# A two-layer block of attention, FP4 feed-forward, Mamba and LoRA: the products of the scan moved from VectorE to TensorE and GpSimd

## The reference

```
A_disc = exp(delta[..., None] * A)
B_x = delta[..., None] * Bm[:, :, None, :] * x1[..., None]
hc = a * hc + b          # a scan over t, for each (d, n)
y = einsum('tbdn,btn->btd', hs, Cm)
```

## Time and profile before

| | |
|---|---|
| median of the three runs | 1017.21 us |
| the profiled execution's own time | 1005.87 us |
| its span | 1003.6 us |
| VectorE busy | 724.7 us, 72% of the span |
| TensorE busy | 692.3 us, 69% |
| ScalarE busy | 461.2 us, 46% |
| GpSimd busy | 153.4 us, 15% |
| chain that ended last | TensorE 37%, VectorE 33%, DMA 11%, ScalarE 8% |

### The profile page before, as it was taken

How to read it: one execution, slowest core, us unless ns; L and a number is a source line. 1 busy time by engine, 2 the same in 40 slices (tenths; PEclk the granted TensorE clock), 3 DMA queues, 4 the chain that set the end, 5 groups by cost and what they waited for, 6 DMA issues and landing times.

```text
span 1003.6 us, 12436 instructions
## 1 busy us (share of the span) xinstructions
PE 692.3 (69%) x4131; PEld 407.2 (41%) x4131; DVE 724.7 (72%) x1295; ACT 461.2 (46%) x931; POOL 153.4 (15%) x265
## 2 busy tenths in 40 slices
PE   3247665786679776877778667956795777855555
PEld 1124344344544444434533454434543453433122
DVE  2716156986789687968897788868896779863951
ACT  2213432662566246634556356625662256436312
POOL 5512013013110412002300230022100000000000
PEclk9997867797889889889979897989898798976775
DMA  4421501361035303350136103520353013002300
GB/s 120 78 54 40 100 1 38 108 139 24 11 99 138 68 0 107 103 103 0 43 120 126 24 11 118 136 48 10 97 133 67 1 47 115 22 0 70 104 0 5
DMA packets 41151, 65.93 MB, mean 66 GB/s; under 512 B 8113, under 2 KB 30338, under 8 KB 38786
## 3 DMA queue, kind: packets, MB, share of 16 engines
q1 hardware_dynamic: 38946, 64.51, 26.0%
q10 hardware_dynamic: 2176, 1.05, 0.6%
HBM read 57.68 MB, written 7.86 MB: 65 GB/s over the span
## 4 chain that ended last, share of the span: by engine, by line
PE 37%; DVE 33%; DMA 11%; ACT 8%; issue 8%; SPq 1%; POOL 0%; DVEq 0%; ACTq 0%
PE ps_s L1052 9%; PE ps_f L1052 8%; DVE shared L1006 6%; PE ps_n L1052 6%; DMA bcrow<-bc_dram 6%; PE ps_y L1052 6%; PE ps_v L1052 6%; DMA x_tm<-in_L_attn_x_dram 5%; DVE mx L893 4%; DVE shared L1000 4%; DVE shared L1011 2%; ACT lmem L757 1%; DVE bn L814 1%; ACT L760 1%; ACT adisc L731 1%
## 5 line engine op out<-in xcount | busy, mean ns | idle before, releaser
L1052 PE MATMUL ps_y<-shared,ident 128*128 128x512 f32 x256 | 146.7, 702 | 52.3 <-DVE shared L1011 52.1
L1052 PE MATMUL ps_s<-stack_mem 72*128 72x128 bf16 (+2 forms) x1280 | 162.9, 248 | 4.8 <-DVE mx L893 4.4
L893 DVE TENSOR_REDUCE mx<-ps_s 128x4 f32<-128x512 f32 x192 | 126.6, 685 | 52.5 <-PE ps_s L1052 49.3
L1006 DVE TENSOR_TENSOR_SCAN shared<-adisc,shared 128x1024 f32<-128x1024 f32 x64 | 146.7, 2292 | 2.2
L1052 PEld LDWEIGHTS ps_s<-stack_mem 72*128 72x128 bf16 (+1 forms) x1280 | 111.1, 106 | 75.6 <-issue 32.0
L649 ACT ACTIVATE probs<-ps_s 128x512 f32<-128x512 f32 x192 | 105.5, 598 | 66.2 <-PE ps_s L1052 64.2
L731 ACT ACTIVATE adisc<-delta,amat 128x255 f32<-128x255 f32 x256 | 108.1, 504 | 39.0 <-DVE shared L1006 28.8
L1052 PE MATMUL ps_s<-causalT,ident_bf 128*128 128x512 bf16 x192 | 83.1, 433 | 23.1 <-DVE mparts L902 14.1
L1000 DVE TENSOR_TENSOR shared<-u,bcrow 128x1024 f32<-128x1024 f32 x64 | 78.0, 1218 | 28.0 <-DMA bcrow<-bc_dram 27.8
L1052 PEld LDWEIGHTS ps_y<-shared,ident 128*128 128x128 f32 x256 | 50.2, 218 | 107.6 <-DVE shared L1011 64.8
L1052 PE MATMUL ps_s<-causal,ident_bf 128*128 128x512 bf16 x128 | 55.3, 432 | 46.7 <-DVE mx L893 36.8
(11 more groups left out here) (213 smaller groups left out, 1114.2 us busy)
## 6 DMA issues: line engine op xcount, KB each, us to landing
bcrow<-bc_dram SPq DMA_DIRECT2D x64, 512.0 KB, 4.2
stack_mem<-stack_dram SPq DMA_DIRECT2D x48, 192.0 KB
stack_mem<-stack_dram SPq DMA_DIRECT2D x144, 64.0 KB
stack_dram<-parts SPq DMA_DIRECT2D x24, 256.0 KB, 2.3
x_tm<-in_L_attn_x_dram ACTq DMA_DIRECT2D x8, 128.0 KB, 11.4
xb<-in_L_attn_x_dram SPq DMA_DIRECT2D x8, 128.0 KB, 2.8
out_dram<-y_out SPq DMA_DIRECT2D x8, 128.0 KB, 2.5
fmem<-in_L_attn_conv_w_dram SPq DMA_DIRECT2D x1, 512.0 KB
```

The lines of the kernel that those rows point to most:

```text
L893: V.tensor_reduce(mx[:, a, i, hd], ps_s[:, n % 2].rearrange("p (h n) -> p h n", n=P), AX.X, ALU.max).then_inc(s_max, 1)
L1006: V.tensor_tensor_scan(hs[:, j % HB].rearrange("p n c t -> p (n c t)"), adisc[:, j % 2].rearrange("p n c t -> p (n c t)"), bx[:, j % 2].re ...
L1052: return nc.tensor.matmul(o, lhsT, rhs, start=start, stop=stop, **kw)
```

## The change

- **u times B.** `mamba` now computes B transposed (tokens on partitions) with six small matmuls, and transposes u by four into `uT`. ScalarE makes, for each state and half of the tokens, a diagonal matrix of B (`diag`, four 128-column activations a step). TensorE multiplies `uT` by the diagonals: 32 fp32 matmuls of 256 columns a turn into `ps_f`, one bank for each half c of the channels (new stream `products`). VectorE scans from PSUM, one instruction of 512 elements for each c, 16 a turn. The product for (j+1, c) waits for the scan of (j, c), as they share the bank.
- **Times C.** One GpSimd product of 1024 elements a step, in place (new stream `scan` on GpSimd). Only C is sent to the partitions, in four DMAs of 512 KB a turn, all issued once the projection is there.
- **Stack.** The 12 loads of the stack's parts per pass become four, each read three times by a broadcast.
- **Maxima and masks.** The first pass takes the second token half against all 256 keys, so that a maximum needs no second operation; the causal matmuls cover only the blocks that need a mask.
- **LoRA.** The 16 token rows go by one DMA to one partition; each correction is four matmuls of one row by one row. GELU reads PSUM with the bias.
- **Smaller ones.** The sum of the two attention outputs is made by TensorE in the transposes; softplus ends in one operation; the table load ahead of each turn is gone.
- **Order.** All lists of `PLAN` are new. All 24 steps of the first pass now lie beside `norm` and `ffn`, the second pass beside `mamba`, except its last `weigh`; the scan has TensorE nearly alone.

The diff, cut to its core; the first lists are those of SyncE, GpSimd, ScalarE, VectorE and TensorE, in this order:

```diff
+        "lora_ffn": [47, 77.8],
+        "core": [57.5, 60, 60.3, 84, 86.5],
+        "prep": [69.4, 69.4, 72.8, 75.2, 91.3, 111.9],
+        "rows": [101.4, 103.5, 103.6, 103.8, 104.1],
...
+        "scan": [85.9, 89.7, 92.7, 96.5, 100, 103.5, 107, 110.4],
...
+        "core": [2.9, 52.9, 54.5, 55.1, 56, 56.5, 57, 57.6, 58.1, 59, 59.5, 60.1, 61, 61.8, 62.4, 62.9, 70.9, 71.4,
+                 72, 75.3, 75.8, 76.4, 77.9, 97, 98.8, 101, 115.4],
+        "norm": [7.4, 9.9],
+        "mamba_out": [12.5],
+        "lora_ffn": [17.2, 32.2, 51.1],
+        "ffn": [25.2, 28.1, 51.6, 55.6],
+        "mamba": [58.6, 61.5, 66.4, 70.5, 72.5, 79.6],
+        "scan": [80.1, 86.9, 88, 92.3, 95.1, 99.1, 102.3, 106],
+        "products": [83.5, 84.7, 85.9, 87.2, 88.4, 91.2, 94.1, 97.6],
...
-        "mamba_out": [3.7, 12.7, 22.2],
-        "norm": [5, 6.8, 8.7],
-        "core": [6, 6.6, 9, 18.4, 20, 20.6, 22.9, 32.7, 33.4, 36.2, 37.6, 41.4, 49.5, 50.3, 51, 53.4, 54, 55.7, 56.4,
-                 57.2, 58.6, 59.6, 60.2, 61, 63, 65.4],
-        "ffn": [11.3, 12.9, 14.3, 15.9, 16.8, 24.7, 27.4, 28.4, 29.5, 31.3, 36.4, 38.2],
...
+        "mamba_out": [1.3, 9.8, 14.4],
+        "norm": [2.2, 5.5, 9.4],
+        "core": [3.2, 3.8, 6.7, 7.3, 13.5, 14.1, 15.8, 16.5, 19.1, 19.7, 20.7, 21.3, 23.2, 24.1, 31.5, 32.1, 35.4,
+                 37, 37.1, 39.4, 40, 43.6, 44.3, 45.7, 46.3, 49.7],
+        "ffn": [14.7, 17.1, 17.5, 18.2, 20.3, 28.3, 32.7, 36.6, 40.7, 44.9, 51.2, 53.1],
+        "prep": [21.9, 23.9],
+        "lora_ffn": [22.6, 27.1, 46.9, 48.6],
+        "mamba": [56.3, 63.2, 72.4],
+        "scan": [82.9, 84.1, 86.1, 87.8, 89.6, 90.8, 93.5, 94.7, 97, 98.2, 100.4, 101.6, 103.9, 105.1, 107.4, 108.6],
...
+        "norm": [0, 2.2, 3.7],
+        "prep": [0.9, 3, 4.5, 6.4, 8.4, 9.5, 33.7],
+        "core": [1.4, 1.9, 4.1, 5.1, 7.3, 7.6, 13.1, 13.7, 16.6, 17.2, 18.7, 19.3, 20.9, 21, 28.7, 29.1, 31.1, 31.7,
+                 33.8, 35, 35.6, 39, 39.6, 43.2, 43.9, 47.2, 47.3, 49.9, 50.2, 50.6, 51, 51.5, 52.2, 52.7, 53, 53.5,
+                 54.1, 54.6, 55, 55.5, 56.1, 57, 57.4, 57.7, 62.7, 63.1, 63.5, 67.7, 68.4, 68.9, 69.2, 71.8, 72.6,
+                 75.2, 75.7, 76, 76.7, 110.3],
+        "mamba_out": [5.5],
+        "lora_ffn": [16.1, 18.5, 24.9, 27, 30.1, 32],
+        "ffn": [19.9, 22.6, 25.8, 26.4, 44.7, 48.5],
+        "mamba": [56.6, 58.4, 64.4, 66.8, 73.5],
+        "products": [80.6, 81.5, 83, 84.8, 86.5, 88.2, 91.3, 92.2, 94.7, 95.6, 98.2, 99.1, 101.7, 102.6, 105.1, 106],
+        "scan": [89.5, 93, 96.5, 100, 103.4, 106.9, 111.7, 114.9],
...
+        shared = sb("shared", [P, 4 * T * HB + 4 * P * DR])
+        hs = shared[:, 0:4 * T * HB].rearrange("p (k c n t) -> p k c n t", k=HB, n=2, c=NC)
+        diag = shared[:, 4 * T * HB:].rearrange("p (k u n t) -> p k u n t", k=DR, u=TT, n=2)
...
+                    sp.dma_start(stack[0:KROWS, 2 + a].rearrange("p h n -> p (h n)"),
+                                 stack_dram[2 + a].rearrange("i (d h) n -> (i d) (h n)", d=DH).unsqueeze(0).to_broadcast([3, 3 * DH, H * T])).then_inc(stack_r[a], 16)
...
+                        sp.dma_start(stack[rows, a].rearrange("p h n -> p (h n)"),
+                                     stack_dram[a, i].rearrange("(d h) n -> d (h n)", d=DH).unsqueeze(0).to_broadcast([3, DH, H * T])).then_inc(stack_r[a], 16)
...
+                sp.wait_ge(dbc_sb, b + 1)
+                sp.dma_start(c_dram, dbc[0:N, :]).then_inc(c_w, 16)
+                for i in range(N // 4):
+                    yield
+                    if i == 0:
+                        sp.wait_ge(c_w, b * 16 + 16)
+                    sp.dma_start(crow[:, 2 * i:2 * i + 2].rearrange("p k n t -> p (k n t)"),
+                                 c_dram[4 * i:4 * i + 4].rearrange("n t -> (n t)").partition_broadcast(P)).then_inc(c_r[i], 16)
...
+                sp.wait_ge(x3_sb, b + 1)
+                sp.dma_start(lrow, x3[1:1 + 4 * LR, 0, :]).then_inc(lr_r, 16)
...
+                for j in steps:
+                    yield
+                    pool.wait_ge(c_r[j // 2], b * 16 + 16)
+                    pool.wait_ge(hs_sb, b * 16 + 2 * j + 2)
+                    h = hs[:, j % HB].rearrange("p c n t -> p c (n t)")
+                    G.tensor_tensor(h, h, crow[:, j].rearrange("p n t -> p (n t)").unsqueeze(1).to_broadcast([P, NC, 2 * T]),
+                                    ALU.mult).then_inc(hc_sb, 1)
...
+                act.wait_ge(uT_ps, b + 1)
+                A(uT[:].rearrange("p u c -> p (u c)"), ps_f[:, 1, :], ACT.Copy).then_inc(uT_sb, 1)
...
+            def products(b):
+
+                for j in range(N // 2):
+                    yield
+                    if j == 0:
+                        act.wait_ge(bT_sb, b + 1)
+                    if j >= DR:
+                        act.wait_ge(bx_ps, b * 16 + 2 * (j - DR) + 2)
+                    for t in range(TT):
+                        for n in range(2):
+                            last = A(diag[:, j % DR, t, n], ident[:], ACT.Identity, scale=bT[:, t, 2 * j + n:2 * j + n + 1])
+                    last.then_inc(diag_sb, 1)
...
-                        last = A(h1T[:, c], ps_n[:, (c % 2) * T:(c % 2 + 1) * T], ACT.Identity, bias=b1c[:, c:c + 1])
-                    last.then_inc(h1_pre, 1)
-                act.wait_ge(h1_pre, b * 2 + 2)
-                A(h1T, h1T, ACT.Gelu).then_inc(h1_sb, 1)
+                        last = A(h1T[:, c], ps_n[:, (c % 2) * T:(c % 2 + 1) * T], ACT.Gelu, bias=b1c[:, c:c + 1])
+                    last.then_inc(h1_sb, 1)
...
-                    V.tensor_reduce(mx[:, a, i, hd], ps_s[:, n % 2].rearrange("p (h n) -> p h n", n=P), AX.X, ALU.max).then_inc(s_max, 1)
+                    V.tensor_reduce(mx[:, a, min(i, 1), hd[0]:hd[-1] + 1:2], ps_s[:, n % 2].rearrange("p (h n) -> p h n", h=len(hd)), AX.X, ALU.max).then_inc(s_max, 1)
...
-                dve.wait_ge(cstd_sb, f * 2 + 2)
-                V.tensor_tensor(comb, cstd[:].rearrange("p t h d -> p t (h d)"), comb, ALU.add).then_inc(comb_sb, 1)
...
-                    last = V.scalar_tensor_tensor(w2e[:, r], ps_n[:, r::RC], lscale[:, 0:1], w2T[:, r], ALU.mult, ALU.add)
-                last.then_inc(weff, 1)
+                V.scalar_tensor_tensor(w2e, ps_n[:].rearrange("p (n r) -> p r n", r=RC), lscale[:, 0:1], w2T[:], ALU.mult, ALU.add).then_inc(weff, 1)
...
+
+                for j in range(N // 2):
+                    for c in range(NC):
+                        yield
+                        dve.wait_ge(bx_ps, b * 16 + 2 * j + c + 1)
+                        dve.wait_ge(ad_sb, b * 16 + 2 * j + c + 1)
+                        if j >= HB:
+                            dve.wait_ge(y_ps, b * 8 + j - HB + 1)
+                        V.tensor_tensor_scan(hs[:, j % HB, c].rearrange("p n t -> p (n t)"),
+                                             adisc[:, j % 2, c].rearrange("p n t -> p (n t)"),
+                                             ps_f[:, c, :], 0.0, ALU.mult, ALU.add).then_inc(hs_sb, 1)
...
+                    if i == 0:
+                        mm(bank, ident_bf[:], causal[:].unsqueeze(1).to_broadcast([P, 4, P]), stop=False)
+                        for c, h in enumerate(hd):
+                            last = mm(bank[:, c * P:(c + 1) * P], stack[0:KROWS, a, h, 0:P],
+                                      stack[0:KROWS, 2 + a, h, 0:P], start=False, stop=(c == 3))
+                    else:
+                        for c, h in enumerate(hd[2 * i - 2:2 * i]):
+                            mm(bank[:, c * T:(c + 1) * T], stack[0:KROWS, a, h, P:T],
+                               stack[0:KROWS, 2 + a, h, :], start=(c == 0), stop=False)
+                        last = mm(bank.rearrange("p (h k n) -> p h k n", k=2, n=P)[:, :, 1], ident_bf[:],
+                                  causal[:].unsqueeze(1).to_broadcast([P, 2, P]), start=False)
...
                         for k in range(2):
                             h = hd[2 * i + k]
-                            last = mm(ps_s[:, n % 3, k * T:(k + 1) * T], stack[0:R, 2 + a, h, 0:P], stack[0:R, a, h, :],
-                                      start=False, stop=(k == 1))
+                            mm(ps_s[:, n % 3, k * T:(k + 1) * T], stack[0:R, 2 + a, h, 0:P], stack[0:R, a, h, :],
+                               start=(k == 0), stop=False)
+                        last = mm(ps_s[:, n % 3, :].rearrange("p (h q n) -> p h q n", q=2, n=P)[:, :, 0], ident_bf[:],
+                                  causalT[:].unsqueeze(1).to_broadcast([P, 2, P]), start=False)
...
-                    last = tr(ps_n[:, t * P:(t + 1) * P], comb[:, t])
+                pe.wait_ge(cstd_sb, f * 2 + 2)
+                for t in range(TT):
+                    for i, part in enumerate((cstd, cgeo)):
+                        last = mm(ps_n[:, t * P:(t + 1) * P], part[:, t].rearrange("p h d -> p (h d)"), ident[:], start=(i == 0), stop=(i == 1))
...
```

(34 more changed lines are left out.)

285 lines of the change are left out of this document (90 added, 195 removed).

## The result

The changed kernel takes 1014.82 us (median of seven runs, 1011.99 to 1017.8); the kernel before, seven runs, 1009.98. The ratio is 1.016, 95% interval 1.010 to 1.022: slower by 1.6%. The forecast was 1000 us, 1.7% faster. Each profiled execution can be set beside the other: 1005.87 us (span 1003.6) before, 1011.99 (span 1010.2) after. The prediction's sum gave 994 for the profiled execution; it took 18 us more.

The account below looks back on a forecast made before the run. VectorE and TensorE were nearly full, neither the bound alone; TensorE would bound the scan. A turn of 50 + 20 + 37.5 = 107.5 against 105.8, with the ends -12 in all: 1005.9 becomes 994, as median 1000 us; range 962 to 1042.

Parts of the forecast that it names:

- C: Stage from u to the next y, with the scan: TensorE becomes its bound, 37.5 us a turn, 12 less.
- B: Stage from rms to u: GELU pass and table load go, second-pass exponentials come in; 20.0 us a turn, 2 less.
- The lead: Start of the scan's stage: chain from u through transposes, copy, decays and first diagonals, 5.2 us; first scan 6 behind u.
- A = 50: Stage from y to rms, 34.2 us before: more maxima and gate operations bring VectorE's work to 40, the length to 50.
- list walk: VectorE's and TensorE's lists stepped through from y: quantised x1 at 18.0 us, hidden product 24.2, rms 48.8.
- a us for locked small operations: Between y and rms: allowance of one us for small operations held up by another engine, included in the 50.
- The rival 'slower': y to rms: hand-overs and TensorE at 1.2 GHz make it 57 us, a turn 114.5, whole 1043 to 1049; chance 0.18.
- The rival 'faster': y to rms near VectorE's 40: filled gaps and 2.4 GHz give 44 us, a turn 101.5, whole 962; chance 0.36.
- GpSimd beside the scan: Scan stage: rival that scans and GpSimd products hold each other up, 7 us a turn, whole 1050; chance 0.06.
- The ends: Outside turns 1 to 5: turn 0 +2 us, turn 6 +5, turn 7 -7, turn 8 -8, start -4.
- The stack costed at nothing: The stack's 24 loads become 8, all landing in time either way: no cost in a middle turn.
- The 6 us that I added: Step from 994 in the profiled execution's frame to the 1000 us median, taking half of the 11 us between them.

Follow-up runs that it names:

- three_gone: Changed kernel with hq_first's swap, GpSimd's six line products on one column each, and warm2's idle matmuls: 978.21 us, ratio 0.973 to the kernel before.
- warm2: Changed kernel with idle TensorE matmuls added in the idle stretches between y and rms, to keep its clock up: 999.69 us, ratio 0.990 to the kernel before.
- four_gone: three_gone with every second first-pass maximum also taken over only 16 scores: 947.69 us, ratio 0.942 to the kernel before.
- pair_sum: Changed kernel with VectorE adding the two states of a scan step, so TensorE adds one tile a step: 998.77 us, ratio 0.995 to the kernel before.
- hq_first: Changed kernel with ScalarE's copy of the transposed hidden layer ahead of the square root of the LoRA's norm: 995.11 us, ratio 0.982 to the kernel before.
- best: Changed kernel with hq_first, pair_sum and the scan's first diagonals moved ahead of u's copy, nothing left out: 973.74 us, ratio 0.964 to the kernel before.
- best_vraw_24: best with ScalarE's gate copy ahead of x3's root and the stack's 24 loads of the kernel before: 983.92 us, ratio 0.976 to the kernel before.
- late geometry: Changed kernel with the second half of the geometry's preparation moved behind rms: 1075.01 us, ratio 1.068 to the kernel before; with 24 stack loads 1082.75 us, 1.073.
- lora_tail_late: Changed kernel with the last part of the LoRA layer moved to the end of the scan's stage: 1039.47 us, ratio 1.034 to the kernel before.
- mx_half: Changed kernel with every second first-pass maximum taken over 16 scores of each row instead of 128 or 256: 988.49 us, ratio 0.976 to the kernel before.

## Why the prediction was wrong

**C and B were right.** TensorE is the bound of the scan, rounds 3.45 instead of 3.68, scans 1.208, no DMA wait. The lead was under-costed: the first product comes 6.2 us behind u, not 5.2, and the first scan 7.4, not 6. The transposes of u, put at 0.9, are done 2.1 us after u's end, as TensorE first finishes a weigh and scores of the second pass; and the diagonals take 0.3 each, not 0.25:

```profile
741.00 1.51 PE L1031 MATMUL ps_v<-probs,vz 128*32 128x256 f32 x16
...
743.26 0.61 PE L1035 MATMUL ps_f<-ident,fmem 128*128 128x128 f32 x4
...
746.02 3.60 ACT L739 ACTIVATE shared<-ident,bT 128x128 f32<-128x128 f32 x12
...
747.34 1.99 PE L1031 MATMUL ps_f<-shared,uT 128*128 128x256 f32 x8 [1.48 <-ACT shared L739]
```

That was made up by the shorter rounds: 37.1 against 37.5. VectorE's busy time in the turn is 69.1 (68 forecast), TensorE's 97.3 (92, at a higher clock).

**The step that failed is A = 50**, in the mean 5.5 us short in each of five turns, 27 us, more than the whole difference of 1000 to 1015. The list walk had most marks right: three_gone, without three terms, quantises x1 at 17.7 (forecast 18.0), starts the hidden product at 25.7 (24.2) and ends A at 49.7. It left out or under-priced three things:

- GpSimd's hold on VectorE, 2.4 us. I had put down "a us for locked small operations", about what the kernel before shows in A (a pair of 1.15 instead of 0.60, an operation of 0.61 instead of 0.17). The lines' products stand where they stood, 6 to 10 us after y; it is VectorE's list that changed beside them. They now meet the refinement of x1's norm too, and their two longest meet the pair behind it, which takes 2.01 us.
- ScalarE's copy behind the LoRA's square root, 1.2. I had named it, but with 5.7 us from the quantised hidden layer to the down-projection, where 6.7 were measured (710.6 to 717.3).
- TensorE at 1.2 GHz for about half of A, 1.6 to 2. In the walk every matmul was at 2.4 GHz.

That three_gone lands on the 50 is in part luck. VectorE's work there is 43.0, not 40, and its idle time 6.7, not 10: two errors that cancel. The sum of the work had left out the LoRA layer's last sum and norm, 2.4 us, which in the kernel before stood behind rms and now stand ahead of it, and had one maximum and one pair behind the maxima too few (13 and two were added, not twelve and one). And three_gone has the copy ahead of the square root, where the walk had it behind.

**The rival 'slower'** named the place, the mechanism and the point (A over 53), and A came out at 55.5. Its price was wrong: some 9 us of matmuls doubled should have given 7 more, they gave some 2 in the mean (net, by warm2), presumably since much of what doubles stands beside VectorE's work. The rest of its 57 came from the other two terms. I gave it 0.18 and the forecast 0.40; what I had no row for, a clock of 1.00 in A once its matmuls wait for maxima one by one, deserved more. The rival 'faster' (A = 44) lost: even four_gone is at 46.4. (Its 962 us should read 958: the other two outcomes are shifted by 6 us, this one by 10.) GpSimd beside the scan cost nothing. By the Trainium skill, GPSIMD Engine Reference, section Key points, GpSimd contends with VectorE instructions in a 2-port perf mode or with two SBUF inputs; these scans have one, the other is in PSUM. The trace agrees (1.208), and also in that VectorE's two-input operations of 0.16 took 0.6 beside GpSimd. In pair_sum the contention is there too, with the other engine paying: the two-input sums took 0.69, and GpSimd's product got 0.36 longer.

**The ends.** Start and turn 0 gave 10.4 us (first y at 220.2 against 230.6), forecast 2: C shortened there like everywhere, while A does not lie behind a y. Turns 1 to 5 cost 19.1 (forecast 0). Turn 6 cost 7.6 (5). Turn 7 gave 1.6 (7): its A is 39.8, not 32, with no maximum in it. There the LoRA layer stands ahead of the feed-forward, and the hidden product comes 22.7 us after y instead of 18.2; hq_first and best bring it down to 37.7 and 35.8. Turn 8 gave 8.2 (8). In all +6.5, and the two spans differ by 6.6. The 6 us that I added from the profiled execution to the median were 2.8.

**The stack costed at nothing** was right for the changed kernel by luck: there the loads end ahead of their use, and best_vraw_24 has the same middle turns with 24 loads. Alone in the kernel before they cost 1.4%.

**Where the gain went.** The scan's products left VectorE and C fell by 12.3 us a turn. TensorE then had no room in C for the second pass of the scores (24 exponentials stood there, now 5); it went to B and the end of A, and pushed the first pass, whose maxima had stood half in B (12, and 1 in C, by the traces of turn 5), wholly ahead of rms. The LoRA layer's end went the same way, and A rose by 18.9. What remained idle is VectorE in B and C (23.4 of 56 us busy), where nothing could use it but sums like that of pair_sum.

**What stays open.** What sets the 46.4 of four_gone, in which VectorE is idle for 8 us and TensorE, its idle matmuls counted as work, for 4; some 2 of VectorE's busy time there is hold (1.97 and 1.87 for two products of 0.89). Why the same idle matmuls brought TensorE's clock back early in some turns and late in others. That GpSimd's hold could be avoided by another place for the lines was tried only together with the late geometry.

## What to carry to other kernels

Work that is moved off a full engine makes room only in the stage where it stood. Look at once which other work must leave that stage because the new bound has no room for it, and cost the stage that receives it by three prices besides the work: an engine that holds up another at that moment, copies in an in-order list behind waits of another chain, and TensorE's clock once it waits in small pieces. Check the first of these again in every variant: a hold can move to another instruction and eat what the variant gained, as in lora_tail_late and mx_half. One swap in a list was worth nearly as much as a whole edit of the scan here (10.1 and 13.5 us by the spans, 20 and 16 by the medians).

## What the hardware showed that was not expected

- Taking 4.1 us of work from TensorE in A lowered its clock there (0.74 to 0.71), and A gained only 0.8, in part because a VectorE product of 0.89 us met GpSimd and took 2.69; adding 8 us of idle matmuls raised the clock to 0.92 and shortened A by 1.6. The same matmuls in best cost 1.9.
- An addition of two SBUF operands on VectorE beside the scan's GpSimd product kept its 0.69 us in all 56 cases, and the product grew from 2.36 to 2.72 on average. Each of these sums had started 0.04 to 0.23 us ahead of the product. A product of two SBUF operands on VectorE that started 0.9 us behind a GpSimd operation went from 0.89 to 2.69 (lora_tail_late). But the pair of scalings of 128 elements went from 0.60 to 2.01, though each of the two had started 0.02 to 0.07 us ahead of a GpSimd product: who pays isn't told by the recorded starts alone.
- Stack loads whose source is repeated three times ran at a DMA share of 0.19 and 80 GB/s, plain ones at 0.56 and 111 GB/s.
